# A first windowed attention with its keys ahead of its values, two of eight products on GpSimd at first, and normalisation on ScalarE

## The chip, the core and the metric

The kernel runs on one core of a Trainium2 chip. The metric is the device time of one launch in microseconds (us). Engines are named as in the profile: PE is TensorE (PEld its weight loads), DVE VectorE, ACT ScalarE, POOL GpSimd, SP SyncE, which here only issues transfers. Each engine works through its own list of instructions in order; semaphores tie the lists together.

## The reference, cut to what matters

Four blocks follow each other: a windowed cross attention, a small mixture of adapters, a latent attention and a routed mixture of experts. The change lies in the first block alone:

```python
def _L0_xattn_ref(x, cond, Wq, bq, Wk, bk, Wv, bv, Wo, bo):   # x, cond: (32, 64, 512) = (B, C, T)
    q = _pointwise(Wq, bq, x); k = _pointwise(Wk, bk, cond); v = _pointwise(Wv, bv, cond)
    k = jnp.pad(k, ((0, 0), (0, 0), (8, 7))); v = jnp.pad(v, ((0, 0), (0, 0), (8, 7)))
    idx = jnp.arange(T)[:, None] + jnp.arange(16)[None, :]
    k_win = k[:, :, idx].reshape(B, H, hd, T, W); v_win = v[:, :, idx].reshape(B, H, hd, T, W)
    dots = jnp.einsum('bhdt,bhdtw->bhtw', qh, k_win) * scale      # H = 8, hd = 8, W = 16
    attn = jax.nn.softmax(dots, axis=-1)
    out = jnp.einsum('bhtw,bhdtw->bhdt', attn, v_win)
    return _pointwise(Wo, bo, out.reshape(B, C, T))
x = x + jnp.tanh(g_xattn[0]) * _L0_xattn_ref(_layernorm(x), ctx_4096, ...)
```

## The kernel before, in words

`window_attention` holds x as 16 tiles of 128 rows (two batches of 64 channels) by 512 positions. Group 0 is tiles 0 to 7, group 1 tiles 8 to 15. A unit is one group at a quarter of the positions (T4 = 128), so there are 8 units, 0 to 7; four use group 0. Per unit:

- PE makes the queries (`queries`, L367, 4 matmuls) in PSUM: one half of a bank for the even tiles, one for the odd. ACT adds the bias, the even half in place in PSUM (L284), the odd half into the SBUF tile `q_p` (L287).
- DVE multiplies queries with shifted keys for the 4 even pairs of shifts (L523, `made`), reading PSUM and SBUF; POOL does the 4 others (L230, `pool_made`), reading only SBUF. They fill the 8 slots of `prod[:, m]`, for the quads m = 0 to 3.
- PE sums over the head's channels (`reduce_dots`, L388, even then odd half); ACT copies the result into `attn` (`take_dots`, L299); DVE takes the running maximum (`peak_of`, L539) and subtracts it (`shift`, L545 and L546, all operands in SBUF); ACT takes the exponential (L304); POOL sums over the window (L236 to L241), DVE inverts (L553), POOL multiplies (L246, `normalise_attn`).
- PE spreads the weights over the head's channels (`spread_attn`, L400, couples (m, k)); DVE multiplies them with shifted values (`weighted`, L533) into `prod[:, m]`; PE multiplies with the output weights (`project(u, m, w, n)`, L367 out_ps, n slices from w); DVE adds into x (`add_out`, L562).

The software pipeline is written out by hand. In round v the engines make the dots of unit v and spread, weigh and project unit u = v - 1, with the last of unit v - 2 in front. The query, dot and spread results share three PSUM banks (`ring_ps`); the list `uses` hands them out, and `take` waits until the one before has been read. Keys and values (`keys_values`, `keep`, L278) are made for group 0 at the start, key and value in turn, and for group 1 inside round 3 (`KV_AFTER`), where DVE also normalises tiles 8 to 15 (`normal`, L104). The context tiles pass through four buffers `cond`, filled by SP (L213) and at first by ACT (L268). PE begins when five small loads (`w_in`) are in: weights, `sel`, `ident`, biases and gates. Statistics of x (L495 to L508) and all 8 normalised tiles of group 0 come before the first queries.

## Time and profile before

| | us |
|---|---|
| median of 3 runs | 1569.11 (1568.35 to 1573.99) |
| the profiled execution's own time | 1558.55 |
| its span | 1556.8 |
| PE, DVE, ACT, POOL busy in the span | 1320.9, 811.0, 420.0, 320.4 |
| first attention, start to last product on PE | 0 to 421.5 |

The busy times are sums over all four blocks, and say little of the first one; the windows below cut it at the moments when the queries of a unit are ready. What an engine waits for, and for how long, stands in brackets at the end of a timeline row. The trace counts each matmul of this kernel twice (an x8 in a row is 4 matmuls of the program).

### The profile page before, as it was taken

The numbers are of one execution on the slowest core, as the hardware profiler recorded it, in microseconds if no ns is written. First come the engines' busy times: TensorE is split into PE (matmuls) and PEld (weight loads), VectorE is DVE, ScalarE is ACT, GpSimd is POOL, SyncE is SP. The second block draws the span as 40 slices with busy tenths as digits, with TensorE's granted clock in tenths as the row PEclk, the third lists the DMA queues.
The fourth block names the chain that finished last, engine by engine and source line by source line (L and its number), as shares of the span: only waits on it lengthen the run. The fifth ranks groups of instructions, "written<-read, shape, count | busy, mean of one in ns | idle before, by whom it ended". The sixth has DMA issues, their size and how long they took to land. (4 is left out here: it accounts for less than half of the span.)

```text
span 1556.8 us, 18857 instructions
## 1 busy us (share of the span) xinstructions
PE 1320.9 (85%) x5849; PEld 655.8 (42%) x5850; DVE 811.0 (52%) x1774; ACT 420.0 (27%) x1161; POOL 320.4 (21%) x194
## 2 busy tenths in 40 slices
PE   4477888888788999899998999899996999899950
PEld 1022222222264555455553555455553333477730
DVE  4577868888674156703573156703575451122224
ACT  4201122111033243223342243223343100144420
POOL 3726536656000000000000000000000025232236
PEclk9679999999989999999999999999998998699985
DMA  5000000000060010001000010000004800355647
GB/s 202 0 1 1 1 28 1 1 1 1 1 244 1 1 28 1 2 0 27 0 0 1 0 27 0 1 0 0 0 0 159 324 0 11 124 164 170 166 149 242
DMA packets 44928, 81.02 MB, mean 52 GB/s; under 512 B 21441, under 2 KB 22177, under 8 KB 44338
## 3 DMA queue, kind: packets, MB, share of 16 engines
q1 hardware_dynamic: 34450, 45.50, 8.6%
q0 software_dynamic: 7424, 21.00, 5.1%
q10 hardware_dynamic: 2976, 13.64, 2.2%
q8 instruction: 30, 0.49, 0.1%
q14 instruction: 48, 0.39, 0.1%
HBM read 59.10 MB, written 21.01 MB: 51 GB/s over the span
## 5 line engine op out<-in xcount | busy, mean ns | idle before, releaser
L1151 POOL DMA_INDIRECT table<-ids,slot_of x32 | 30.9, 965 | 897.4 <-DVE slot_of L1362 887.9
L926 PE MATMUL big_ps<-wo_sb,ot 128*128 128x512 f32 x384 | 176.2, 594 | 7.6 <-DVE ot L1040 7.6
L533 DVE TENSOR_TENSOR prod<-ring_ps,v_c 128x1024 f32<-128x1024 f32 x128 | 151.7, 1215 | 43.1 <-PE ring_ps L400 42.8
L917 PE MATMUL big_ps<-ht,wq_sb 128*128 128x512 f32 x384 | 171.4, 592 | 0.0
L883 ACT ACTIVATE probs<-s_ps,npeak 128x128 f32<-128x128 f32 x256 | 91.6, 362 | 270.1 <-PE p_ps L973 233.3
L230 POOL TENSOR_TENSOR prod<-q_p,k_c 128x2048 f32<-128x2048 f32 x32 | 133.4, 4202 | 82.4 <-ACT q_p L287 82.4
L400 PE MATMUL ring_ps<-attn,sel 32*128 32x512 f32 x512 | 100.4, 675 | 47.2 <-DVE prod L533 31.1
L367 PE MATMUL out_ps<-prod,w 64*64 64x512 f32 x1024 | 130.5, 629 | 0.0
L388 PE MATMUL ring_ps<-prod,sel 128*32 128x512 f32 x512 | 72.7, 668 | 34.3 <-POOL prod L230 17.2
L917 PEld LDWEIGHTS big_ps<-ht,wq_sb 128*128 128x128 f32 x384 | 70.1, 190 | 73.9 <-issue 72.8
L926 PEld LDWEIGHTS big_ps<-wo_sb,ot 128*128 128x128 f32 x384 | 68.0, 190 | 72.9 <-issue 65.2
L996 DVE COPY v<-big_ps 128x384 f32<-128x384 f32 x32 | 17.8, 557 | 152.0 <-PE big_ps L909 152.0
L1497 PE MATMUL u_ps<-wr,xgt 128*128 x384 | 92.7, 385 | 0.0
L1038 DVE COPY ot<-o_ps 96x192 f32<-96x192 f32 x128 | 44.5, 348 | 89.9 <-PE o_ps L980 89.6
L1040 DVE COPY ot<-o_ps 32x64 f32<-32x64 f32 x384 | 84.6, 220 | 5.1
L909 PE MATMUL big_ps<-wv_sb,ht 128*128 128x384 f32 x256 | 85.9, 486 | 0.0
L961 PEld LDWEIGHTS s_ps<-kt,qt 96*128 96x128 f32 x512 | 76.8, 191 | 20.1 <-ACT qt L863 8.4
L944 PE MATMUL big_ps<-ht,wk_sb 128*128 128x512 f32 x192 | 85.1, 603 | 0.0
L980 PE MATMUL o_ps<-probs_t,v 128*96 128x256 f32 x256 | 78.5, 388 | 5.2 <-ACT probs_t L891 2.3
L961 PE MATMUL s_ps<-kt,qt 96*128 96x128 f32 x512 | 78.4, 275 | 5.1 <-ACT qt L863 5.1
L523 DVE TENSOR_TENSOR prod<-ring_ps,k_c 128x2048 f32<-128x2048 f32 x32 | 72.4, 2288 | 19.3 <-ACT ring_ps L284 14.8
L1017 DVE TENSOR_REDUCE npeak<-s_ps 128x2 f32<-128x256 f32 x128 | 54.2, 423 | 50.8 <-PE s_ps L961 47.0
(193 smaller groups left out, 1811.8 us busy)
## 6 DMA issues: line engine op xcount, KB each, us to landing
wr<-in_w_routed ACTq DMA_DIRECT2D x4, 3072.0 KB, 21.4
y_rows<-y_sb SPq DMA_DIRECT2D x48, 256.0 KB, 2.0
X<-in_x SPq DMA_DIRECT2D x4, 1024.0 KB, 7.3
ht<-in_ctx_t SPq DMA_DIRECT2D x16, 256.0 KB, 4.9
out<-X SPq DMA_DIRECT2D x16, 256.0 KB, 2.8
cond<-in_ctx SPq DMA_DIRECT2D x12, 256.0 KB, 2.9
wq_sb<-in_wq SPq DMA_DIRECT2D x1, 3072.0 KB, 14.7
wo_sb<-in_wo SPq DMA_DIRECT2D x1, 3072.0 KB, 21.7
```

Source lines behind the costliest of these rows:

```text
L230: nc.gpsimd.tensor_tensor(prod[:, m, 4:8], over_shifts(q_p[:], 4), shifts(k_c, 1, 4, v % 4, m), ALU.mult).then_inc(pool_made, 1)
L367: last = nc.tensor.matmul(out[rows[1 - b if crossed else b], :], w_sb[rows[b], w, rows[b]], rhs[rows[b]], start=start, stop=stop)
L400: last = nc.tensor.matmul(bank("b", u, m, k)[:, j, :], spread[strip, k // 2, :], attn[strip, u % 2, 4 * m:4 * m + 4, :], start=True, stop= ...
L533: V.tensor_tensor(prod[:, m, 2 * k:2 * k + 2], bank("b", u, m, k)[:, :, :].rearrange("p j (w t) -> p j w t", w=4), shifts(v_c[:, u // 4], ...
L883: nc.scalar.activation(probs[:, u % 3, g2, :], s_ps[u % 2][:, g2 * P:(g2 + 1) * P], ACT.Exp, bias=npeak[:, u % 3, g2:g2 + 1], accum_out=to ...
L909: last = nc.tensor.matmul(ps[:, 0:KV * HD1], ht[:, c, b], wv_sb[:, c, :], start=(c == 0), stop=(c == CH - 1))
L917: last = nc.tensor.matmul(ps[:, :], wq_sb[:, c, (a * HC + k) * P:(a * HC + k + 1) * P], ht[:, c, :, 1, :], start=(c == 0), stop=(c == CH - 1))
L926: last = nc.tensor.matmul(ps[:, :], ot[:, a % 2, c, k * P:(k + 1) * P], wo_sb[:, a * HC + c, :], start=(c == 0), stop=(c == HC - 1))
L944: last = nc.tensor.matmul(ps[:, :], wk_sb[:, c, k // 2 * P:(k // 2 + 1) * P], ht[:, c, k % 2 * 4:k % 2 * 4 + 4], start=(c == 0), stop=(c = ...
L961: last = nc.tensor.matmul(s_ps[u % 2][:, g2 * P:(g2 + 1) * P], qt[:, a % 2, b, 2 * g2:2 * g2 + 2], kt[:, a, b], start=True, stop=True)
L1040: last = nc.vector.tensor_copy(ot[HD1:P, a % 2, c, t], heads[c * PIECE:(c + 1) * PIECE, HC])
L1497: last = nc.tensor.matmul(u_ps[m % 2][:, 0:2 * INTER], xgt[:, m % 2, c, :], wr[:, bass.ds(e, 1), c * 2 * INTER:(c + 1) * 2 * INTER], start ...
```

## The change

1. **Start.** SP issues weights, x tiles 0 to 7, and then the whole context of group 0 in four transfers into `first_cond`, which is `prod[:, 3]` under another name; then `sel`, `ident`, four tiles of group 1's context, x tiles 8 to 15. ACT issues only biases and gates. PE waits for the weights alone. It makes four key products, the queries of unit 0, and then the four values; a new wait keeps DVE and POOL off `prod[:, 3]` until the values are made (`kv_done` 8).
2. **Normalisation.** DVE normalises only the first 128 columns of tiles 0 to 7 (xn_ready); ACT does the other 384 with scale and a new `minus_mean` after the values are kept, and all of tiles 8 to 15 between the `take_dots` of unit 3.
3. **Units 0 and 1.** POOL takes 2 of the 8 pairs (128x1024), DVE the other 6: a 128x2048 product and an extra 128x1024 product from PSUM (`made_extra`). ACT biases the odd half in two pieces.
4. **Round 1.** `invert(0)` and `sum_up(0)` change places with a product, and the `shift` of unit 1 comes before the weighted products of unit 0.
5. **Every round from 1.** Slices of `project` move: two slices of m = 1 each time where one stood, then one slice of m = 2, the last spread, the next queries, and only then the second slice of m = 2.

```diff
-            for n in range(4, TILES):
-                if n == PAIRS: ...
-                sp.wait_ge(kv_done, n // 2 * 2 - 2)
-                sp.dma_start(cond[:, n % 4, :], ctx[n]).then_inc(cond_in[n % 4], 16)
+            for i in range(4):
+                sp.dma_start(first_cond[:, 2 * i:2 * i + 2, :],
+                             ctx[2 * i:2 * i + 2].rearrange("t p d -> p t d")).then_inc(first_in[i], 16)
...
@@ gpsimd
-                nc.gpsimd.tensor_tensor(prod[:, m, 4:8], over_shifts(q_p[:], 4), shifts(k_c, 1, 4, v % 4, m),
-                                        ALU.mult).then_inc(pool_made, 1)
+                if v == 0 and m == QUADS - 1:
+                    pool.wait_ge(kv_done, 8)
+                n = 2 if v < 2 else 4
+                nc.gpsimd.tensor_tensor(prod[:, m, 8 - n:8], over_shifts(q_p[:, 4 - n:4], n),
+                                        shifts(k_c, 9 - 2 * n, n, v % 4, m), ALU.mult).then_inc(pool_made, 1)
...
@@ scalar
+            def normal(t, first):
+                nc.scalar.activation(xn[:, t % PAIRS, first:], X[:, t, first:], ACT.Identity, bias=minus_mean[:, t:t + 1],
+                                     scale=rstd[:, t:t + 1]).then_inc(rest_ready, 1)
             root(0)
             for i in range(4):
                 keep("k", 0, i)
+            queries(0)
+            for i in range(4):
                 keep("v", 0, i)
-            queries(0)
+            for t in range(PAIRS):
+                normal(t, T4)
...
@@ tensor
             for i in range(4):
                 keys_values("k", 0, i)
+            queries(0)
+            for i in range(4):
                 keys_values("v", 0, i)
-            queries(0)
...
                 other_keys_values(2, 1)
-                project(u, 1, 0, 1)
+                project(u, 1, 0, 2)
                 spread_attn(u, (2, 3), (3, 0))
                 other_keys_values(2, 3)
-                project(u, 1, 1, 1)
+                project(u, 1, 2, 2)
                 spread_attn(u, (3, 1), (3, 2))
                 other_keys_values(3, 1)
-                project(u, 1, 2, 2)
                 project(u, 2, 0, 1)
                 spread_attn(u, (3, 3))
                 if v + 1 < UNITS:
                     queries(v + 1)
+                project(u, 2, 1, 1)
...
@@ vector
+                if v < 2:
+                    dve.wait_ge(q_ready, 2 * v + 2)
+                    extra = bank("q", v)[:, 1, 0:2 * T4].rearrange("p (j t) -> p j t", j=2)
+                    V.tensor_tensor(prod[:, m, 4:6], over_shifts(extra, 2), shifts(k_c, 1, 2, v % 4, m), ALU.mult)\
+                     .then_inc(made_extra, 1)
...
-                    for m in range(1, QUADS):
-                        dot_products(v, m)
+                    dot_products(v, 1)
+                    dot_products(v, 2)
                     invert(0)
+                    dot_products(v, 3)
                     for m in range(1, QUADS):
                         peak_of(v, m)
+                    shift(v)
+                    dve.wait_ge(kv_ready, 8)
                     weighted(u, 0, 0, 1, 2, 3)
-                    shift(v)
...
-                    if v == 3:
-                        if m == 1:
-                            dve.wait_ge(q_done, 4)
-                        for t in ((8, 9, 10), (11, 12, 13), (14, 15))[m - 1]:
-                            normal(t)
```

At the start of PE's list the group's context was multiplied in one run (cond, 8 products of 4 matmuls), before:

```order
L367 MATMUL ring_ps<-cond,w 64x512 x32
L367 MATMUL ring_ps<-xn,w 64x512 x4
L388 MATMUL ring_ps<-prod,sel 32x512 x24
L367 MATMUL ring_ps<-xn,w 64x512 x4
L388 MATMUL ring_ps<-prod,sel 32x512 x40
```

Now (the prod read by L399 is `first_cond`):

```order
L399 MATMUL ring_ps<-prod,w 64x512 x16
L399 MATMUL ring_ps<-xn,w 64x512 x4
L399 MATMUL ring_ps<-prod,w 64x512 x16
L428 MATMUL ring_ps<-prod,sel 32x512 x24
L399 MATMUL ring_ps<-xn,w 64x512 x4
L428 MATMUL ring_ps<-prod,sel 32x512 x40
```

The queries of unit 0 stand after 16 matmuls in place of 32. On DVE, the dots of units 0 and 1 stood so before:

```order
L523 TENSOR_TENSOR prod<-ring_ps,k_c 128x2048
L539 TENSOR_TENSOR peak<-ring_ps,peak 128x512
L545 TENSOR_TENSOR peak<-peak 128x256
L545 TENSOR_TENSOR peak<-peak 128x128
L546 TENSOR_TENSOR attn<-attn,peak 128x2048
L523 TENSOR_TENSOR prod<-ring_ps,k_c 128x2048 x3
L553 RECIPROCAL inverse<-total 128x128
L539 TENSOR_TENSOR peak<-ring_ps,attn 128x512
L539 TENSOR_TENSOR peak<-ring_ps,peak 128x512 x2
L533 TENSOR_TENSOR prod<-ring_ps,v_c 128x1024 x4
```

Now, from the last product of unit 1's first quad (L564 and L568 are its two pieces) to the shift of unit 1:

```order
L568 TENSOR_TENSOR prod<-ring_ps,k_c 128x1024
L585 TENSOR_TENSOR peak<-ring_ps,peak 128x512
L591 TENSOR_TENSOR peak<-peak 128x256
L591 TENSOR_TENSOR peak<-peak 128x128
L592 TENSOR_TENSOR attn<-attn,peak 128x2048
L564 TENSOR_TENSOR prod<-ring_ps,k_c 128x2048
L568 TENSOR_TENSOR prod<-ring_ps,k_c 128x1024
L564 TENSOR_TENSOR prod<-ring_ps,k_c 128x2048
L568 TENSOR_TENSOR prod<-ring_ps,k_c 128x1024
L599 RECIPROCAL inverse<-total 128x128
L564 TENSOR_TENSOR prod<-ring_ps,k_c 128x2048
L568 TENSOR_TENSOR prod<-ring_ps,k_c 128x1024
```

Each quad costs DVE a second instruction, and the reciprocal stands one quad earlier. On PE, the last part of round 2 (spreads of unit 1, its projections, the queries of unit 3) stood so before:

```order
L367 MATMUL out_ps<-prod,w 64x512 x16
L400 MATMUL ring_ps<-attn,sel 128x512 x8
L367 MATMUL out_ps<-prod,w 64x512 x4
L400 MATMUL ring_ps<-attn,sel 128x512 x4
L367 MATMUL out_ps<-prod,w 64x512 x4
L400 MATMUL ring_ps<-attn,sel 128x512 x4
L367 MATMUL out_ps<-prod,w 64x512 x12
L400 MATMUL ring_ps<-attn,sel 128x512 x2
L367 MATMUL ring_ps<-xn,w 64x512 x4
L400 MATMUL ring_ps<-attn,sel 128x512 x2
L367 MATMUL out_ps<-prod,w 64x512 x8
```

Now:

```order
L399 MATMUL out_ps<-prod,w 64x512 x16
L440 MATMUL ring_ps<-attn,sel 128x512 x8
L399 MATMUL out_ps<-prod,w 64x512 x8
L440 MATMUL ring_ps<-attn,sel 128x512 x4
L399 MATMUL out_ps<-prod,w 64x512 x8
L440 MATMUL ring_ps<-attn,sel 128x512 x4
L399 MATMUL out_ps<-prod,w 64x512 x4
L440 MATMUL ring_ps<-attn,sel 128x512 x2
L399 MATMUL ring_ps<-xn,w 64x512 x4
L399 MATMUL out_ps<-prod,w 64x512 x4
L440 MATMUL ring_ps<-attn,sel 128x512 x2
L399 MATMUL out_ps<-prod,w 64x512 x8
```

The 12 matmuls of projection that stood right ahead of the last spread and the queries are 4 now; 4 each have moved behind the two spreads before, and 4 behind the queries.

## Rows read from the trace of the kernel before

**Rows 1.** Windows by unit: PE, PEld, DVE, ACT, POOL busy (instructions), PE clock, DMA
```profile
47.86:115.24 67.38, 41.58 (x212) 9.86 (x212) 48.60 (x48) 8.71 (x10) 35.38 (x14) 0.71 0.00 1
162.60:222.02 59.42, 46.18 (x330) 12.84 (x328) 46.03 (x37) 14.43 (x17) 26.32 (x9) 0.94 0.05 18
222.02:262.77 40.75, 35.64 (x266) 9.53 (x264) 34.83 (x29) 5.52 (x9) 26.01 (x9) 1.00 0.01 2
...
348.37:421.50 73.13, 65.73 (x502) 18.42 (x500) 55.09 (x50) 4.86 (x7) 26.01 (x9) 1.00 0.00 1
```
**Rows 2.** Windows of 2 us at the start, same columns, last GB/s
```profile
10.00:12.00 2.00, 0.00 (x0) 0.00 (x0) 0.38 (x4) 0.00 (x0) 0.00 (x0) 1.00 1.04 392
...
24.00:26.00 2.00, 1.93 (x20) 0.55 (x12) 0.00 (x0) 1.73 (x2) 0.00 (x0) 1.00 1.04 395
```
**Rows 3.** Timeline: start us, us, engine, line, operation, count, [idle before <-releaser]
```profile
12.59 2.47 DVE L495 BATCH_NORM_STATS2 bn<-X 128x6 f32<-128x512 f32 x4 [2.18 <-DMA X<-in_x]
...
13.18 6.65 PE L367 MATMUL ring_ps<-cond,w 64*64 64x512 f32 x32 [13.18 <-DMA ident<-in_ident_in]
...
16.20 3.74 DVE L104 TENSOR_SCALAR xn<-X,mv,rstd 128x512 f32<-128x512 f32 x8
...
26.28 0.66 ACT L284 ACTIVATE ring_ps<-ring_ps,b 128x512 f32<-128x512 f32 x1
...
27.03 6.69 DVE L523 TENSOR_TENSOR prod<-ring_ps,k_c 128x2048 f32<-128x2048 f32 x3 [6.97 <-ACT ring_ps L284]
...
47.95 2.29 DVE L523 TENSOR_TENSOR prod<-ring_ps,k_c 128x2048 f32<-128x2048 f32 x1 [5.29 <-ACT ring_ps L284]
```
**Rows 4.** Timeline of DVE in unit 1
```profile
50.87 2.13 DVE L545 TENSOR_TENSOR peak<-peak 128x256 f32<-128x256 f32 x1
...
53.04 4.15 DVE L545 TENSOR_TENSOR peak<-peak 128x128 f32<-128x128 f32 x1
...
82.06 0.69 DVE L539 TENSOR_TENSOR peak<-ring_ps,peak 128x512 f32<-128x512 f32 x1 [7.91 <-ACT attn L299]
...
115.28 6.88 DVE L523 TENSOR_TENSOR prod<-ring_ps,k_c 128x2048 f32<-128x2048 f32 x3 [0.51 <-ACT ring_ps L284]
```
**Rows 5.** Timeline: DVE's normalisation in unit 3
```profile
188.16 4.75 DVE L104 TENSOR_SCALAR xn<-X,mv,rstd 128x512 f32<-128x512 f32 x3
...
200.98 5.55 DVE L104 TENSOR_SCALAR xn<-X,mv,rstd 128x512 f32<-128x512 f32 x3
...
216.80 0.99 DVE L104 TENSOR_SCALAR xn<-X,mv,rstd 128x512 f32<-128x512 f32 x2
```
**Rows 6.** Timeline: the last part of unit 4, the first of unit 5
```profile
253.03 1.14 PE L400 MATMUL ring_ps<-attn,sel 32*128 32x512 f32 x8 [0.38 <-DVE prod L533]
...
256.09 1.14 PE L400 MATMUL ring_ps<-attn,sel 32*128 32x512 f32 x8 [0.91 <-DVE prod L533]
257.16 2.81 PE L367 MATMUL out_ps<-prod,w 64*64 64x512 f32 x24
...
260.95 1.09 PE L367 MATMUL ring_ps<-xn,w 64*64 64x512 f32 x8
...
262.81 6.88 DVE L523 TENSOR_TENSOR prod<-ring_ps,k_c 128x2048 f32<-128x2048 f32 x3 [0.51 <-ACT ring_ps L284]
...
282.37 0.68 DVE L539 TENSOR_TENSOR peak<-ring_ps,peak 128x512 f32<-128x512 f32 x1
```
**Rows 7.** Groups by shape, first 430 us: busy, mean ns, idle before
```profile
L533 DVE TENSOR_TENSOR prod<-ring_ps,v_c 128x1024 f32<-128x1024 f32 x128 | 151.7, 1215 | 43.1 <-PE ring_ps L400 42.8
L230 POOL TENSOR_TENSOR prod<-q_p,k_c 128x2048 f32<-128x2048 f32 x32 | 133.4, 4202 | 82.4 <-ACT q_p L287 82.4
...
L546 DVE TENSOR_TENSOR attn<-attn,peak 128x2048 f32<-128x2048 f32 x8 | 18.3, 2292 | 0.3
...
L307 ACT ACTIVATE X<-X,gated_bias 128x512 f32<-128x512 f32 x16 | 10.3, 716 | 0.0
...
L278 ACT ACTIVATE k_c<-ring_ps,b 128x1024 f32<-128x1024 f32 x8 | 8.9, 1111 | 3.2 <-PE ring_ps L367 3.1
```

More of the change, by code:

```diff
@@ L133, in window_attention @@
         peak = sb("peak", [P, WINDOW // 4, T4])
+        minus_mean = sb("minus_mean", [P, TILES])
         total, inverse = sb("total", [P, T4]), sb("inverse", [P, T4])
@@ L141, in window_attention @@
                     (2, 3): (("v", 2), ("k", 3)), (3, 1): (("v", 3),)}
-        uses = [((k, 0, i), 0) for i in range(4) for k in "kv"]
-        uses += [(("q", 0), 0), (("d", 0, 0), 0), (("d", 0, 1), 0), (("q", 1), 1)]
+        uses = [(("k", 0, i), 0) for i in range(4)] + [(("q", 0), 0)]
+        uses += [(("v", 0, 0), 0), (("v", 0, 1), 0), (("v", 0, 2), 1), (("v", 0, 3), 1)]
+        uses += [(("d", 0, 0), 1), (("d", 0, 1), 1), (("q", 1), 1)]
         for v in range(1, UNITS + 1):
@@ L171, in bank @@
             return ring_ps[bank_of[use]]
-        kv_at = {key: n for n, key in enumerate([(k, g, i) for g in range(2) for i in range(4) for k in "kv"])}
-        w_in, x_in, cond_in = sem("w_in"), [sem(f"x_in{k}") for k in range(4)], [sem(f"cond_in{k}") for k in range(4)]
+        kv_order = [(k, 0, i) for k in "kv" for i in range(4)] + [(k, 1, i) for i in range(4) for k in "kv"]
+        kv_at = {key: n for n, key in enumerate(kv_order)}
+        w_in, bias_in, sel_here = sem("w_in"), sem("bias_in"), sem("sel_here")
+        x_in, first_in, cond_in = ([sem(f"{n}{k}") for k in range(4)] for n in ("x_in", "first_in", "cond_in"))
         pads, tanh_done, bias_ready, x_biased = sem("pads"), sem("tanh_done"), sem("bias_ready"), sem("x_biased")
@@ L371, in keys_values @@
             def keys_values(k, g, i):
-                n = g * PAIRS + 2 * i
-                for j in range(2):
-                    pe.wait_ge(cond_in[(n + j) % 4], 16 * ((n + j) // 4 + 1))
+                if g == 0:
+                    pe.wait_ge(first_in[i], 16)
+                    even, odd = first_cond[:, 2 * i, :], first_cond[:, 2 * i + 1, :]
+                else:
+                    for j in range(2):
+                        pe.wait_ge(cond_in[2 * (i % 2) + j], 16 * (i // 2 + 1))
+                    even, odd = cond[:, 2 * (i % 2), :], cond[:, 2 * (i % 2) + 1, :]
                 ps = take(k, g, i)
-                both(ps[:, 0, :], ps[:, 1, :], 1 + (k == "v"), cond[:, n % 4, :], cond[:, (n + 1) % 4, :]).then_inc(kv_done, 1)
+                both(ps[:, 0, :], ps[:, 1, :], 1 + (k == "v"), even, odd).then_inc(kv_done, 1)
             def queries(v):
-                if v % 4 == 0:
-                    pe.wait_ge(xn_ready, PAIRS * (v // 4 + 1))
+                if v == 0:
+                    pe.wait_ge(xn_ready, PAIRS)
+                else:
+                    pe.wait_ge(rest_ready, PAIRS * (v // 4 + 1))
                 ps = take("q", v)
@@ L386, in reduce_dots @@
                 pe.wait_ge(pool_made if odd else made, 4 * v + m + 1)
+                if odd and v < 2:
+                    pe.wait_ge(made_extra, 4 * v + m + 1)
                 for j in range(4):
```

75 lines of the change are left out of this document (48 added, 27 removed).

## The prediction, written before the changed kernel ran

> **What bounds the kernel now.** I read first the windows by unit [rows 1]. The first attention takes 421.5 us of the 1556.8 us span and nothing behind it is edited, so the sum is made in it. Three kinds of stretch stand there. Units 4 and 5 take 40.75 us each; PE is busy for 35.64 and DVE for 34.83 of it, so neither is full: they hand work to and fro. Unit 3 takes 59.4 us and unit 1 67.4 us, with PE busy for 46.2 and 41.6 and a mean granted clock of 0.94 and 0.71 (1.2 GHz is 0.5, 2.4 GHz is 1). These have most idle time.
>
> Then the timeline at the start [rows 3]. The queries of unit 0 stand behind eight key and value products, and those behind a DMA wait that ends at 13.18 with `ident`. DVE waits 6.97 us for ACT and begins its products at 27.03. In unit 1 [rows 4] the shift of unit 0 is held up: two small operations take 2.13 and 4.15 us, and DVE's last maximum waits 7.91 us for ACT, PE and POOL behind it. In unit 3 [rows 5] DVE normalises eight tiles in 11.3 us; the last two take 0.99 us, so six of the eight were slowed from about 0.5 to 1.6 us or more while POOL worked. In unit 4 [rows 6] PE waits 0.38 and 0.91 us for DVE's weighted products, and then does 2.81 us of projection ahead of the last spread and the queries for which DVE waits next.
>
> **The change part by part.**
>
> *Start.* Two queues together moved 392 GB/s and one alone 395 [rows 2], so one queue for all costs no rate, and what counts is the order of bytes. Before, 3.6 MB were in at 12.6. Now x tiles 0 to 7 and the weights are the first 2.4 MB. By the rate they are in at about 9.4, not 12.59, and the four context parts of 0.52 MB (1.35 us each) at 10.7, 12.1, 13.4, 14.7. PE's first 32 passes took 6.65 us, so a key product takes 1.66 us at the clock of the start: 10.8 to 17.4 for four, and the queries are ready on PE at 18.6. Normalisation keeps pace: from the landing to the first tile were 3.6 us [rows 3]; plus 0.2 for `minus_mean` and eight tiles of 128 columns at 0.2, it ends at 14.8. An eighth of the 3.74 us, 0.47, is the upper bound for a tile, and a quarter of it the lower; both end ahead of the queries. ACT keeps the last keys until 18.7 (1.11 us [rows 7]) and has the even queries at 19.5. First product: 27.03 to 19.5, 7.5 us.
>
> From there DVE has per quad one product at 2.23 us (6.69 for three) and one extra of 128x1024. The nearest row for that is the weighted product, also PSUM times SBUF: 1.215, 1.14 when back to back [rows 7]. Its bounds are that and the whole 2.29 of a 128x2048; I take the lower, since shape and operands are the same. So 3.35 per quad. The first scores wait on ACT behind the values (4 x 1.11) and eight normalisations of 384 columns. Three quarters of 0.716 is 0.54 [rows 7], 4.3 us in all; bounds 2.9 and 5.7. They end at about 29, the second scores leave ACT at 31.6, so DVE stands for 2 us ahead of the fourth quad. The fourth product ends at 35.8, unit 0's last scores are out at 37.5, two bias operations later (1.3) ACT biases the queries of unit 1: ready at 39.5. Its product starts at 39.6 and not at 47.95: **8.4 us** gained.
>
> ScalarE's cost is stated by the Trainium skill (page ScalarE: Activation LUTs, Rules for kernel authors) as about 0.3 us plus 0.83 ns an element. By that an operation of 384 columns takes 0.62 us, eight take 5.0, and this term would be 0.7 us smaller; the row of 716 ns for 512 columns agrees with the rule's 0.72.
>
> *Unit 1.* Before, 47.95 to 82.75, 34.8 us. Now DVE has four quads (13.4), four maxima (0.69 each [rows 4], 2.8), the reciprocal (1.0, an estimate: an eighth of the elements of a 128x1024 product, but a division) and the shift (2.3 [rows 7], with its two small parts 3.0). POOL's instructions are half as long, 2.1 in place of 4.2 (bounds 2.1 and 4.2), and a small part is held until the one running ends, so the two wait 1.0 and 1.9 us. With 1.2 us until the query's second half and the sum of unit 0 are there, and 2.5 us of waiting for the last scores, it ends 25.0 us later, at 64.6: **9.8 us** gained. Should a held operation be passed over by POOL, this falls by 2.
>
> The cause is seen in the rows: operations of 128x256 and 128x128 take 2.13 and 4.15 us beside POOL, products with one operand in PSUM keep 2.23. The Trainium skill (page SBUF - State Buffer, Who interferes with whom) says that a `tensor_tensor` with both inputs in SBUF and GpSimd's reads shut each other out for a whole instruction. By that rule the extra products, which read PSUM, are free of it, as summed; if they too were held, 2.1 us each for eight would take 17 us back, and no row shows that.
>
> *Rest of round 1.* Before, 82.75 to 115.28 (32.5). The new order makes the shift first, so exponential and sum of unit 1 come early, but they were not late; what is late is PE, at the low clock, whose spreads (1,0) to (1,2) now wait for the weighted products of quad 0. I get 34.5: **2.0 lost**. Queries of unit 2: 16.2 us earlier.
>
> *Projections (round 2 on).* In unit 4, replayed with its own durations [rows 6]: 8 more passes (0.86 us) ahead of the spread at 253.03, of whose time 0.38 was waiting: 253.45. 16 passes behind it end at 256.4, where it was 256.09. Then 8 passes in place of 24 ahead of the last spread, and the queries start at 259.45 and not 260.95. DVE must first weigh its last couple, done at 261.1; its product starts at 261.3, not 262.81: 1.5 us. In the next part POOL's four products (16.8) set the end; DVE's last maximum moved from 282.37 by 1.9, as it stood then behind PE and DVE work of its own. So 1.9 us per round: units 4 and 5 give 3.7, round 6 with the head of 7 gives 1.9 (statistics on DVE hide part of it), round 2 gives 2.0. At the end PE is bound (65.7 of 73.1 us [rows 1]); the waits filled there, 1.3 and 0.8, give 2.1. **9.7 us**.
>
> *Unit 3.* With DVE free of 11.3 us [rows 5], PE's 46.2 us bound it. Through the banks in their order: spread (1,3) at 191.7, (2,1) at 195.3, (2,3) at 200.6, (3,1) at 205.9, (3,3) at 208.8, queries ready on PE at 210.8 and on ACT at 211.5, where they were ready at 222.02 [rows 1]: 10.5, and 0.3 from the head of the round. **10.8 us**. On ACT the eight normalisations (0.72 each) stand between scores 4 to 5 us apart and end ahead of the exponential: hidden. If that cover failed, up to 1.4 us. The waits for context tiles 12 to 15 are on the same products as before.
>
> *Sum*: 8.4 + 9.8 - 2.0 + 9.7 + 10.8 = 36.7. From the profiled execution's 1558.55 (span 1556.8) that is 1521.9. The median of plain runs stood 10.6 above it, so the forecast is **1532.5**.
>
> **Rivals.**
> 1. *PE's clock holds in units 1 and 2.* PE waits less, so 41.6 us of work at a mean of 0.71 might run near 1. Then some 8 us more go, as the low clock doubles a pass (0.21 against 0.10 us, by 6.65 for 32 and 1.93 for 20). For: less idle time. Against: DVE still sets the pace there. 45 us gained: 1524.
> 2. *The moved projections give nothing*: spreads are pushed back by them and DVE's weighted products wait as long as was won. For: each moved slice stands in front of a spread that DVE needs. Against: PE waited there already. 27 us: 1542.
> 3. *The dots of units 0 and 1 become DVE's bound*: extra products at their upper bound (1.1 us more each, eight: 9) and scores held on ACT behind normalisation (another 6). 21 us: 1548.
> 4. *Slower.* In units 4 to 7 the slices moved forward leave PE one longer stop behind the queries, and the granted clock drops there to 1.2 GHz. Each us of work at that level costs another us. The 36.7 us are spent when one whole unit's PE work (35.64) has dropped, and with two the kernel takes 1604. For: unit 1's 0.71 and unit 3's 0.94. Against: units 4 and 5 were granted 1.00 with 5 us of idle time each, and the new order has less.
>
> **How the numbers follow.** Forecast (31 to 42 us) 0.58, rival 1 0.16, rival 2 0.12, rival 3 0.10, rival 4 0.04. The range leaves out rival 4 and the far ends of 1 and 3: 1519 to 1550. A measurement of this kernel can tell about 0.5%, 7.8 us, from no change. Rivals 1 to 3 and the forecast are all beyond it; of rival 4 half is slower by more, a quarter within, so faster 0.96, same 0.02, slower 0.02.
>
> **What would show it.** Start: PE's first product at about 10.8, DVE's first product at 19.5. Unit 1: its first product near 39.6, the two small operations of the shift at 1.4 and 2.2 us, last maximum near 64, unit 2's first product near 99. Unit 3: no L104 on DVE, 48.5 us long. Units 4 and 5: 38.9 us and 2 us less PE waiting. The end of the first attention near 385. Later parts: same lengths as before. It would be wrong if products of 128x1024 from PSUM took clearly more than 1.2 us beside POOL, if the context landed after 17, or if units 4 and 5 stayed at 40.7.

## The result, and the profile of the changed kernel

Four runs of the changed kernel gave a median of 1528.43 us (1521.83 to 1535.02), four of the kernel before on the same chip 1568.73: a ratio of 0.9736 (95% interval 0.9685 to 0.9786). The forecast was 1532.5. The profiled execution of the changed kernel is the longest of its four, 1535.02 (span 1533.2), and that of before lies 10 us under its own median. From profile to profile only 23.5 us are gone, from median to median 40.3. The last product of the first attention on PE ends at 383.3 (expected near 385, before 421.4). I therefore read the first attention, where the change lies, apart from what follows.

The windows by unit, with the columns of [rows 1]:

```profile
39.38:96.65 57.27, 39.02 (x216) 9.24 (x216) 50.59 (x52) 8.86 (x11) 27.45 (x14) 0.76 0.00 1
141.84:191.92 50.08, 46.72 (x332) 12.87 (x328) 34.95 (x29) 20.10 (x24) 26.08 (x9) 0.93 0.07 22
191.92:230.88 38.96, 35.70 (x268) 9.46 (x264) 34.66 (x29) 5.53 (x9) 26.07 (x9) 1.00 0.01 2
269.87:311.95 42.08, 37.41 (x268) 9.76 (x264) 38.62 (x37) 5.53 (x9) 26.06 (x9) 0.96 0.00 1
```

Unit 1 (first row) lost 10 us and POOL's part of it went from 35.38 to 27.45. Unit 3 lost 9.3, and PE is busy for 46.72 of its 50.08: it has by far the most work there now. Unit 4 has PE's same 35.7 us of work in 38.96. Unit 6 (last row) is the one with the statistics on DVE, and its clock is 0.96.

The timeline at the start, which answers to [rows 3]:

```profile
10.01 2.44 DVE L536 BATCH_NORM_STATS2 bn<-X 128x6 f32<-128x512 f32 x4
...
11.34 5.59 PE L399 MATMUL ring_ps<-prod,w 64*64 64x512 f32 x32 [11.34 <-DMA prod<-in_ctx]
...
13.68 2.13 DVE L625 TENSOR_SCALAR xn<-X,mv,rstd 128x128 f32<-128x128 f32 x8
...
18.90 2.29 DVE L564 TENSOR_TENSOR prod<-ring_ps,k_c 128x2048 f32<-128x2048 f32 x1 [2.96 <-ACT ring_ps L296]
...
21.11 1.22 DVE L568 TENSOR_TENSOR prod<-ring_ps,k_c 128x1024 f32<-128x1024 f32 x1
...
23.88 4.89 ACT L325 ACTIVATE xn<-X,minus_mean,rstd 128x384 f32<-128x384 f32 x8
...
28.94 0.59 ACT L314 COPY attn<-ring_ps 128x512 f32<-128x512 f32 x1 [0.17 <-ACT xn L325]
...
31.26 0.69 DVE L585 TENSOR_TENSOR peak<-ring_ps,attn 128x512 f32<-128x512 f32 x1 [2.28 <-ACT attn L314]
...
39.46 2.29 DVE L564 TENSOR_TENSOR prod<-ring_ps,k_c 128x2048 f32<-128x2048 f32 x1 [3.46 <-issue]
```

PE starts at 11.34 (expected 10.8) and DVE's products at 18.90 (19.5). An extra product of 128x1024 out of PSUM takes 1.22 us. ACT's eight normalisations take 0.61 us each. The copy of the first scores begins 0.17 us behind them, and DVE stands 2.28 us for it ahead of its first maximum. Unit 1's first product is at 39.46 (39.6).

The timeline of unit 1 and of the rest of round 1, which answers to [rows 4]:

```profile
40.21 6.66 POOL L244 TENSOR_TENSOR prod<-q_p,k_c 128x1024 f32<-128x1024 f32 x3 [11.81 <-ACT q_p L302]
...
43.52 3.50 DVE L591 TENSOR_TENSOR peak<-peak 128x256 f32<-128x256 f32 x2
47.05 2.29 DVE L592 TENSOR_TENSOR attn<-attn,peak 128x2048 f32<-128x2048 f32 x1
...
63.98 0.69 DVE L585 TENSOR_TENSOR peak<-ring_ps,peak 128x512 f32<-128x512 f32 x1 [1.98 <-ACT attn L314]
...
74.48 4.74 PE L399 MATMUL out_ps<-prod,w 64*64 64x512 f32 x32
...
96.69 2.29 DVE L564 TENSOR_TENSOR prod<-ring_ps,k_c 128x2048 f32<-128x2048 f32 x1 [0.51 <-ACT ring_ps L296]
```

The two small operations of the shift take 3.50 us together (expected 1.4 and 2.2), beside POOL instructions of 2.2. The last maximum ends at 64.67 (64.6), and waits 1.98 us where it waited 7.91. A 32-pass projection takes 4.74 us at a mean granted clock of 0.76, where 3.66 is the time at full clock. Unit 2's first product is at 96.69 (99).

### The profile page after: what moved, and what is told of

It reads as the page before. It is cut to its first block and busy times, and to the rows that moved or that the text cites. A ratio compares the mean times of both kernels' runs of the same rounds, so it can differ in the third digit from the quotient of the medians.

```text
span 1533.2 us, 18890 instructions
## 1 busy us (share of the span) xinstructions
PE 1322.0 (86%) x5849; PEld 656.1 (43%) x5850; DVE 804.3 (52%) x1776; ACT 430.3 (28%) x1179; POOL 302.9 (20%) x194
## 5 line engine op out<-in xcount | busy, mean ns | idle before, releaser
L244 POOL TENSOR_TENSOR prod<-q_p,k_c 128x2048 f32<-128x2048 f32 (+1 forms) x32 | 117.9, 3715 | 66.2 <-ACT q_p L302 66.0
L399 PE MATMUL out_ps<-prod,w 64*64 64x512 f32 x1024 | 130.2, 623 | 0.0
L564 DVE TENSOR_TENSOR prod<-ring_ps,k_c 128x2048 f32<-128x2048 f32 x32 | 72.1, 2284 | 14.1 <-ACT ring_ps L296 6.1
```

Of the source, the lines that this page charges most:

```text
L244: nc.gpsimd.tensor_tensor(prod[:, m, 8 - n:8], over_shifts(q_p[:, 4 - n:4], n), shifts(k_c, 9 - 2 * n, n, v % 4, m), ALU.mult).then_inc(po ...
L399: last = nc.tensor.matmul(out[rows[1 - b if crossed else b], :], w_sb[rows[b], w, rows[b]], rhs[rows[b]], start=start, stop=stop)
```

## The experiments

All are single edits of the changed kernel unless said otherwise. I compare the end of the first attention, which is the issue of the first route load on SyncE's queue: 428.69 before, 390.65 in the changed kernel, 391.92 in a second profile of it. Two profiles of one kernel, of which there are two pairs, agree to 1.3 and 1.7 us there. Differences below 2 us are therefore read from the place of the edit alone, and that has a spread too: in the six profiles whose edit does not touch the start, unit 1's queries are ready between 38.4 and 39.9. The end also holds short drops of the granted clock, of 1.6 or 3.3 us, that come and go: eleven profiles have the new order of projections, and in seven of them one of units 4 and 5 has such a drop (mean granted clock 0.96 or 0.92, 40.6 or 42.3 us in place of 39.0). The first profile of the changed kernel has none there, so where an experiment has one, it is named below. Ratios are to the kernel before, measured on the same chip in the same batch.

**The old order of projections.**

```diff
-                    project(old, 2, 2, 2)
+                    project(old, 2, 1, 2)
-                    project(old, 3, 0, 1)
+                    project(old, 2, 3, 1)
-                    project(old, 3, 1, 1)
+                    project(old, 3, 0, 2)
...
+                    project(old, 2, 1, 1)
...
-                project(u, 1, 0, 2)
+                project(u, 1, 0, 1)
...
-                project(u, 1, 2, 2)
+                project(u, 1, 1, 1)
...
+                project(u, 1, 2, 2)
-                project(u, 2, 1, 1)
-            project(UNITS - 1, 2, 2, 2)
+            project(UNITS - 1, 2, 1, 3)
```

> The changed kernel with PE's order of projections as before (one slice ahead of each spread, three ahead of the last one and the queries); all else as changed. In the changed kernel's trace the first attention ends at 390.65 us (start of the next block's first load). Theory: each round from 2 on loses the 1.5 to 1.9 us that the moved slices gave, units 4 and 5 go back from 38.97 to 40.75 us, the end comes at 400.3 (9.7 later). Rival (the moved slices give nothing, the spreads were only pushed back): 390 to 393.

Measured: end at 404.93, 14.3 us later; ratio 0.9823 (0.9776 to 0.9871). Units 4 and 5 took 42.50 and 42.43, which is longer than in the kernel before. Unit 4 and one projection in it:

```profile
193.06:235.56 42.50, 37.28 (x266) 9.88 (x264) 34.75 (x29) 5.51 (x8) 26.08 (x9) 0.96 0.00 1
215.49:220.80 5.31, 5.31 (x38) 1.53 (x36) 4.45 (x4) 1.91 (x1) 2.24 (x1) 0.68 0.00 0
```

The same projection in the changed kernel:

```profile
213.88:217.54 3.66, 3.66 (x38) 1.19 (x36) 3.66 (x4) 1.91 (x1) 0.58 (x1) 1.00 0.00 0
```

The granted clock was 0.68 in that stretch and not 1.00, and the 1.65 us by which the projection is longer are most of what unit 4 has above its 40.75 of before. I repeated the kernel to see whether this belongs to it.

> The same kernel as the first experiment (projections in the order of before), once more. Its first attention ended at 404.93 us, 14.3 later than the changed kernel's, where 9.7 was expected, and units 4 and 5 took 42.5 us each, with a short drop of PE's clock in every unit, where the kernel before took 40.75 with none. If the drops belong to this order and its timing, they are there again and the end is near 405; if they come and go from run to run, units 4 and 5 take 40.75 and the end is near 400.5.

Measured: end at 406.66, 16.0 later (against the first profile of the changed kernel); ratio 0.9853 (0.9785 to 0.9921). Unit 4 again took 42.51, unit 5 now 40.80, and a drop stood behind unit 6 instead. So the drops come and go between executions, and the old order without one gives the 40.8 of before. Against the lengths of the kernel before, the first profile has drops of 1.75, 1.66 and 1.76 us (in units 4 and 5 and behind unit 6), the second of 1.76 and 3.45 (in unit 4 and behind unit 6), 5.2 us in each. Without them, undoing the order costs 9.1 and 10.8 us.

**The projections alone, in the kernel before** (the edit above the other way round, nothing else).

> The kernel before with only the new order of projections on PE. Theory: units 4 and 5 at 38.9 in place of 40.75, the first attention 9.7 us shorter than 428.69, ending at 419, if PE's clock drops as often. Rival (the new order needs the rest of the change): less than 3 us shorter.

Measured: end at 413.50, 15.2 us earlier than before; ratio 0.9900 (0.9845 to 0.9955).

```profile
157.06:214.51 57.45, 46.83 (x332) 13.01 (x328) 45.96 (x37) 14.44 (x17) 26.31 (x9) 0.94 0.06 19
214.51:253.41 38.90, 35.67 (x268) 9.37 (x264) 34.76 (x29) 5.53 (x9) 26.01 (x9) 1.00 0.00 1
```

Unit 4 (second row) is at 38.90, as summed. The 15.2 fall on round 1 with 1.9, unit 2 with 3.6, unit 3 (first row) with 2.0, units 4 and 5 with 3.7, unit 6 with 2.3 and the rest with 1.7. In this pair of profiles the part is worth 15, not 9.7: it also pays in round 1 and in unit 3, where I had not booked it under this head, and in unit 2 more than I had booked. Undone in the changed kernel it was worth 9.1 and 10.8 without the drops. Its size is open between 9 and 15; that it pays 1.8 to 1.9 us a unit is shown by units 4 and 5 of the undisturbed profiles.

**GpSimd with four of eight pairs again in units 0 and 1.**

```diff
-                n = 2 if v < 2 else 4
+                n = 4
...
-                if v < 2:
-                    nc.scalar.activation(odd[:, 0:2 * T4], odd[:, 0:2 * T4], ACT.Identity, bias=b_sb[:, 0:1])
...
-                    V.tensor_tensor(prod[:, m, 4:6], over_shifts(extra, 2), shifts(k_c, 1, 2, v % 4, m), ALU.mult)\
-                     .then_inc(made_extra, 1)
```

> The changed kernel with POOL doing four of the eight pairs in units 0 and 1 too (no extra products on DVE). Theory, by the hold-up of operations with both operands in SBUF: the two small parts of unit 0's shift wait for POOL operations of 4.2 us (together 6 us, not 3.5), the large part starts 4 to 7 us later than 47.05, unit 1's last maximum ends near 70 (64.67 now) and the first attention near 398. Rival (the gain of unit 1 comes from the order of round 1 alone): under 2 us later than 390.65.

Measured: end at 400.57, 9.9 later; ratio 0.9786 (0.9727 to 0.9846). Unit 1 took 64.95 us and began 1.7 later, so unit 2's queries were ready 9.4 later. Behind that, a drop in unit 4 (40.60 us) added 1.6, and other units gave back 1.1. The shift of unit 0 on DVE:

```profile
44.10 6.33 DVE L580 TENSOR_TENSOR peak<-peak 128x256 f32<-128x256 f32 x2
50.47 6.14 DVE L581 TENSOR_TENSOR attn<-attn,peak 128x2048 f32<-128x2048 f32 x1
```

POOL beside it:

```profile
41.77 12.69 POOL L244 TENSOR_TENSOR prod<-q_p,k_c 128x2048 f32<-128x2048 f32 x3 [4.61 <-ACT q_p L300]
```

POOL's three products run from 41.77 to 54.46, at 4.2 us each. The two small operations take 6.33, and the large subtraction 6.14: it ends at 56.61, which is 2.15 behind the third product, so it was held until that had ended. In the changed kernel POOL's three short products end at 46.87 and the subtraction, from 47.05, takes its bare 2.29. That is 12.5 us in place of 5.8. The Trainium skill (page SBUF — State Buffer, Who interferes with whom) says that operations with both inputs in SBUF and GpSimd's reads shut each other out: these rows agree. By the same rule the changed kernel's extra products, which read PSUM, are free of it. They are: the first of them, at 21.11, took 1.22 us while POOL's products ran from 19.71 to 28.40, as it did anywhere else.

**VectorE normalises in unit 3 again.**

```diff
-                    if v == 3:
-                        if m == 0:
-                            act.wait_ge(shift_ready, 2)
-                            act.wait_ge(q_done, 4)
-                        normal(PAIRS + 2 * m, 0)
-                        normal(PAIRS + 2 * m + 1, 0)
...
+                    if v == 3:
+                        if m == 1:
+                            dve.wait_ge(q_done, 4)
+                        for t in ((8, 9, 10), (11, 12, 13), (14, 15))[m - 1]:
+                            normalise(nc, xn[:, t % PAIRS, :], X, t, mv, rstd).then_inc(rest_ready, 1)
```

> The changed kernel with tiles 8 to 15 normalised on DVE in round 3, as before, and not on ACT. Theory: six of the eight operations are held by POOL again (about 10 us on DVE in place of 4), unit 3 takes 57 to 59 us in place of 50.1, the first attention ends near 399. Rival (unit 3 is bound by PE's key and value products anyway): under 2 us later than 390.65.

Measured: end at 397.69, 7.0 later; unit 3 took 58.48; ratio 0.9826 (0.9775 to 0.9877). The normalisation on DVE:

```profile
165.58 4.76 DVE L104 TENSOR_SCALAR xn<-X,mv,rstd 128x512 f32<-128x512 f32 x3
...
178.41 5.56 DVE L104 TENSOR_SCALAR xn<-X,mv,rstd 128x512 f32<-128x512 f32 x3
...
194.82 0.99 DVE L104 TENSOR_SCALAR xn<-X,mv,rstd 128x512 f32<-128x512 f32 x2
```

These are the rows of before [rows 5] to 0.01 us, and unit 3 is back at nearly its old length. By itself this edit is worth 7.0 to 8.4 us, the second figure by unit 3 alone.

**Values between keys again** (`k` and `v` products by turns, queries of unit 0 last; the loads of the change kept).

```diff
-        uses = [(("k", 0, i), 0) for i in range(4)] + [(("q", 0), 0)]
-        uses += [(("v", 0, 0), 0), (("v", 0, 1), 0), (("v", 0, 2), 1), (("v", 0, 3), 1)]
-        uses += [(("d", 0, 0), 1), (("d", 0, 1), 1), (("q", 1), 1)]
+        uses = [((k, 0, i), 0) for i in range(4) for k in "kv"]
+        uses += [(("q", 0), 0), (("d", 0, 0), 0), (("d", 0, 1), 0), (("q", 1), 1)]
```

> The changed kernel with keys and values of group 0 made in turn and the queries of unit 0 behind all eight, as before; loads, normalisation and everything else as changed. Theory: DVE's first product moves from 18.90 to 24 us (4 more products at 1.66 and less), but the first scores stand behind ACT's normalisation, which ends at nearly the same time, so the first product of unit 1 moves only from 39.46 to 42.2 and the end of the first attention by 2.7, to 393.4. Rival (the queries' lead is worth all of itself): 5 us later, 395.7.

Measured: end at 392.37, 1.7 later; ratio 0.9765 (0.9716 to 0.9814).

```profile
22.12 2.29 DVE L561 TENSOR_TENSOR prod<-ring_ps,k_c 128x2048 f32<-128x2048 f32 x1 [6.63 <-ACT ring_ps L295]
...
39.98 2.29 DVE L561 TENSOR_TENSOR prod<-ring_ps,k_c 128x2048 f32<-128x2048 f32 x1 [3.13 <-issue]
```

The products start 3.2 us later, but unit 1 only 0.5. Keys ahead of values is nearly worthless as it stands: what DVE gains at its first product it gives back ahead of the maximum, behind ACT's normalisation (a wait of 2.28 us in the changed kernel, none here). The 1.7 us of the end are no loss of this order either: unit 2's queries were ready 1.2 us earlier, and unit 5 had a drop (42.33 us, 3.3 more).

**VectorE normalises all of group 0.**

```diff
-            for t in range(PAIRS):
-                normal(t, T4)
...
-                V.tensor_scalar(xn[:, t, 0:T4], X[:, t, 0:T4], mv[:, t, 0:1], rstd[:, t:t + 1], ALU.subtract,
-                                ALU.mult).then_inc(xn_ready, 1)
+                normalise(nc, xn[:, t, :], X, t, mv, rstd).then_inc(xn_ready, 1)
```

> The changed kernel with tiles 0 to 7 normalised whole on DVE before the first queries (3.7 us in place of 2.1), nothing of them on ACT. Theory: the first queries start 0.8 us later, but the first scores no longer stand behind 4.9 us of normalisation on ACT, and DVE's stop of 2.3 us ahead of its first maximum goes, so that unit 1's first product comes 1.5 us earlier than 39.46 and the first attention ends near 389. Rival (ACT's share pays, as it takes 1.6 us off the path to the first queries): 1 us later, 391.7.

Measured: end at 387.05, 3.6 *earlier*; ratio 0.9771 (0.9703 to 0.9839).

```profile
25.25 0.59 ACT L314 COPY attn<-ring_ps 128x512 f32<-128x512 f32 x1 [1.16 <-PE ring_ps L425]
...
36.87 2.29 DVE L561 TENSOR_TENSOR prod<-ring_ps,k_c 128x2048 f32<-128x2048 f32 x1 [3.12 <-issue]
```

The first scores leave ACT at 25.25 and not at 28.94, and unit 1 starts 2.6 us sooner, while DVE's first product moved from 18.90 only to 19.01. So that part of the change costs 2.6 us at unit 1's first product: it took work off DVE at a time when DVE was waiting for PE. How much of it reaches the end is open. At unit 2's queries 1.2 are left; units 2 and 3 were then 2.7 and 1.3 shorter, and a drop in unit 4 took 1.6.

**ACT's normalisation dealt out between the scores, and bias operations moved to unit 1.**

```diff
-            for t in range(PAIRS):
+            for t in range(2):
...
+                    if v == 0 and m == 3:
+                        queries(1)
...
+                    if v == 0 and m < 2:
+                        for t in range(2 + 3 * m, 5 + 3 * m):
+                            normal(t, T4)
```

> A version meant to be faster: the changed kernel with ACT's list of unit 0 in another order. Scores of quads 0 and 1 are taken between the normalisations (2, 3 and 3 tiles), the queries of unit 1 get their bias ahead of the last scores, and the output bias is added in unit 1. Theory: DVE's stop of 2.3 us ahead of its first maximum and the one of 3.5 us ahead of unit 1 go; unit 1's first product at 34 in place of 39.46 and the first attention ends 5 to 6 us earlier, near 385. Rival (PE or POOL takes over in unit 1): under 2 us earlier.

Measured: end at 388.15, 2.5 earlier; median 1524.15, ratio 0.9690 (0.9615 to 0.9765).

```profile
33.63 2.29 DVE L567 TENSOR_TENSOR prod<-ring_ps,k_c 128x2048 f32<-128x2048 f32 x1
...
243.84 3.73 PE L443 MATMUL ring_ps<-attn,sel 32*128 32x512 f32 x12 [1.52 <-DVE peak L588]
...
247.51 5.25 PE L402 MATMUL out_ps<-prod,w 64*64 64x512 f32 x32
```

Unit 1's first product is at 33.63, 5.8 us sooner, and unit 2's queries 7.2 sooner. Then 4.7 are given back, 3.3 in unit 5 and 1.3 in unit 6. Unit 5 took 42.30 and not 38.99. Its twelve-pass spread took 3.73 us and the projection behind it 5.25, where 3.66 is the time at full clock; the granted clock in these 8.9 us was 0.61:

```profile
243.84:252.70 8.86, 8.86 (x46) 3.06 (x46) 6.30 (x6) 1.91 (x1) 3.71 (x3) 0.61 0.01 2
```

**The same, and one more slice of projection behind a spread.**

```diff
-                project(u, 0, 0, 4)
+                project(u, 0, 0, 3)
...
+                project(u, 0, 3, 1)
```

> A version meant to be faster: the kernel with scores taken between normalisations, and in each round the fourth slice of the projection of quad 0 moved behind the spread (1,3), (2,0). Theory: PE's wait of 1.4 us per round is partly filled and DVE's 0.3 us goes, 0.3 us per round and 2 us in all; units 4 and 5 at 38.7 without a drop of PE's clock, unit 2's first product at 89.5, end between 381 and 386, by how often the clock drops. Rival (DVE sets these parts alone): 38.96, end as the version it starts from.

Measured: end at 382.75, the earliest of all; units 4 and 5 took 38.82 and 38.84. The slice is worth 0.14 us a unit (0.3 was expected); the rest is the edit above without its drop in unit 5, though with one of 1.6 behind unit 6. The median of 1518.64 (ratio 0.9708, 0.9660 to 0.9757) is the lowest in its batch, 12 us under the repeat of the changed kernel there. The intervals of the two overlap, so in whole time it is likely faster, not shown to be. In the first attention its gain is 8 to 9 us between single profiles.

**Round 1 in the old order** (three dot products ahead of the reciprocal, weighted products ahead of the shift).

```diff
-                    dot_products(v, 1)
-                    dot_products(v, 2)
+                    for m in range(1, QUADS):
+                        dot_products(v, m)
...
-                    dot_products(v, 3)
...
-                    shift(v)
...
+                    shift(v)
```

> The changed kernel with round 1 in its old order: the reciprocal of unit 0 behind all products of unit 1 on DVE, the sum and the normalisation on POOL one product earlier, and the shift of unit 1 behind the weighted products of quad 0. Theory: normalisation of unit 0 ends later (reciprocal at 60 in place of 56.5) and the first spread with it, end of the first attention 1.5 us later, 392.2. Rival (this order is what gained unit 1): 5 us or more later.

Measured: end at 391.31, 0.7 later, which is within what two profiles differ by; ratio 0.9806 (0.9748 to 0.9864). Unit 2's queries were ready at 100.16 and not at 96.65, which is 3.5 later. Units 2 and 3 were then 2.7 and 1.4 shorter, and a drop in unit 4 (40.58 us) took 1.6. Unit 2's length differs by as much among the other experiments (42.5 to 45.2 us), and unit 3 was short here because it had no drop. So nothing shows that the edit itself gives the 3.5 back, and nothing shows that it keeps it: its worth stays open between 0 and 3.5 us.

**The loads as before** (`sel` and `ident` ahead of the context, and the context on two queues).

```diff
-            for i in range(4):
-                sp.dma_start(first_cond[:, 2 * i:2 * i + 2, :],
-                             ctx[2 * i:2 * i + 2].rearrange("t p d -> p t d")).then_inc(first_in[i], 16)
...
+            for i in range(2):
+                act.dma_start(first_cond[:, 2 * i:2 * i + 2, :],
+                              ctx[2 * i:2 * i + 2].rearrange("t p d -> p t d")).then_inc(first_in[i], 16)
...
+            pe.wait_ge(sel_here, 32)
```

> The changed kernel with its first loads as before: half of the group's context from ACT's queue beside the x tiles on SP's, and PE waiting for sel and ident too. Theory: the first key product starts at 13.2 and not at 11.34, the second half of x lands 2.6 us later and the normalised tiles with it, first product on DVE at 21, unit 1's at 41.5, end of the first attention 2.1 us later, 392.8. Rival (loads are hidden behind ACT's normalisation): under 0.7 us later.

```profile
13.54 5.06 PE L403 MATMUL ring_ps<-prod,w 64*64 64x512 f32 x32 [13.54 <-DMA ident<-in_ident_in]
...
20.95 2.29 DVE L567 TENSOR_TENSOR prod<-ring_ps,k_c 128x2048 f32<-128x2048 f32 x1 [2.04 <-ACT ring_ps L299]
```

PE starts 2.2 us later, DVE 2.05, unit 1 1.7. That is the worth of this edit at the start; at unit 2's queries 0.75 of it is left. The end is at 396.18, 5.5 later, of which 4.6 are drops in units 5 and 6 (42.3 and 43.4 us); ratio 0.9826 (0.9772 to 0.9881).

**The changed kernel again, in five rounds.** The profile behind the first attention had asked for it. Between the load of `xt` and the first rows of the routed block, the changed kernel:

```profile
1281.54:1332.11 50.57, 44.60 (x88) 17.91 (x87) 8.40 (x16) 4.63 (x12) 7.75 (x9) 0.56 0.27 84
```

and the kernel before:

```profile
1320.11:1356.46 36.35, 30.23 (x73) 14.49 (x73) 6.02 (x12) 4.63 (x12) 7.80 (x9) 0.58 0.38 116
```

This piece of unedited code took 14.2 us more, and PE was busy for 14.4 more in it. But it is not the same work: 88 matmul records lie in it and 73 before. The load that marks its start does not wait for all of PE's work ahead of it, and PE was further behind by then. From the first load of the routed block to the first rows, where both profiles have the same 396 matmul records, it is 185.3 us against 171.7, 13.7 more, with PE busy for 153.1 and 148.7. PE had stood still ahead of the load, and its granted clock was 0.50 from then to 1321:

```profile
1279.68 0.57 ACT L1226 COPY gt<-y_ps 17x512 f32<-17x512 f32 x1 [24.36 <-remote]
...
1280.40 2.05 PE L1289 MATMUL y_ps<-w_sb,h_sb 128*128 128x512 f32 x2 [9.54 <-ACT gt L1226]
```

Either the change makes this part longer, or its length changes by chance.

> The changed kernel itself once more, for its first attention against its whole time. Theory: the first attention again ends within 1.5 us of 390.65, the stretch of the routed block's shared part that ran 51 us at PE's low clock in the first profile has another length here, and the plain runs spread over more than 10 us; their median is 36 to 42 us under the kernel before. Rival (the change itself lengthens the late low stretch, by 14 us): it is 51 us again, and the plain runs are never more than 30 us under the kernel before.

Measured: median 1530.7 against 1566.9; ratio 0.9769 (0.9714 to 0.9823). Between the load of `xt` and the first rows this profile had 41.5 us, but only because the load of `xt` came late, 8.5 us behind the load of the table that stands just ahead of it:

```profile
1282.37 0.32 SPq L1185 DMA_DIRECT2D tab_sb<-table  x1
1290.88 0.35 SPq L1187 DMA_DIRECT2D xt<-in_b_routed  x1
```

From the load of the table it is 50.0 us, as in the first profile (50.9), and from the start of the block 185.1 (185.3). So the changed kernel had the long form twice (and in this profile a drop in unit 5, 40.62 us). Measured from the start of the block, the 14 profiles fall into two groups: 168.9 to 172.2 us (the kernel before; the old projections, second time; projections alone; four pairs on POOL; values between keys; the loads as before) and 181.9 to 185.3 (the eight others). The old projections have one of each, 183.1 and 168.9 us from the same kernel. So one kernel can have both lengths. The plain times of the changed kernel fit that: three of the six lie at 1519 to 1525 us and three at 1536 to 1538. That the change makes the long form more frequent is not excluded by the traces, but the medians, 36 and 40 us apart, show no such loss against the 38.0 of the first attention. What starts the long form is open: waits of the kind shown above, with `remote` as the releaser, stand in profiles of both groups.

## Why the prediction was right, step by step

The mechanism held: the gain is in the first attention, 38.0 us against a sum of 36.7, and no part of it turned into a new wait of its size. The forecast time of 1532.5 lies 4.1 us above the median. It took the distance from the profiled execution to the median, 10.6 us, over from the kernel before; in the changed kernel the profile lies 6.6 above its median and not below it. It had the long form of the routed block, and the profile of before the short one. That the whole time came out so near rests in part on luck. In the sum itself the two largest errors, 2.5 us too little for the rest of round 1 and 1.5 too much for unit 3, partly cancel. The terms, as measured between the two profiles:

| term | forecast | profiles | undone or done alone |
|---|---|---|---|
| start to unit 1's first product | 8.4 | 8.5 | loads 1.7, keys first 0.5, ACT normalising −2.6 |
| unit 1 to its last maximum | 9.8 | 9.6 | four pairs on POOL 9.4 (units 0 and 1) |
| rest of round 1 | −2.0 | +0.5 | order of round 1: 0 to 3.5 |
| projections, without unit 3 | 9.7 | 10.1 | 13.2 alone; 9.1 and 10.8 undone without drops, unit 3 within |
| unit 3 | 10.8 | 9.3 | VectorE normalising 7.0 to 8.4 |

*Start.* The total was right by errors that cancel. PE began 0.5 us late, and its first 32 passes took 5.59 us and not 6.65: passes of 0.21 us gave way to passes of 0.12 within them and not behind them. I had called the slow ones the low clock, also in rival 1. That rests on their length alone, as the profile lists a granted clock of 1.00 for this stretch in both kernels; that the lowered clock doubles a pass is shown by the spread of 1.99 and 3.68 us under *Unit 3*. And ACT's eight normalisations took 4.89 and not 4.3: three quarters of the 512-column row is too low, as the cost has a part that doesn't shrink with the columns. The Trainium skill's rule (page ScalarE: Activation LUTs, Rules for kernel authors), 0.3 us plus 0.83 ns an element, gave 0.62 for one; the row has 0.61. The rule was better than my scaling.

*Unit 1.* Extra products took 1.22 (bounds 1.14 to 2.29), the small operations 3.5 together (marks 3.6), and the last maximum ended 0.1 us off its mark. That mark was luck in part: the terms as I listed them add up to 26.8 us and not to the 25.0 that I wrote, and 25.2 was measured, as the waits were shorter (0.46 us in place of 1.2 ahead of the reciprocal, 1.98 in place of 2.5 for the last scores). Rival 3 falls with its larger half: the extra products stayed at the row of same shape and operands. Its smaller half, scores held on ACT behind normalisation, is there in part, with the 2.6 us that VectorE normalising group 0 gives back.

*Rest of round 1.* A mis-sized term. I let PE run at the low clock throughout, but this stretch had a mean granted clock of 0.82 already before (0.84 now), and 32 passes took 4.74 us at 0.76. That the assumed clock made up all of the 2.5 us between −2.0 and +0.5 is argued, not measured. Over unit 1 the clock rose from 0.71 to 0.76: rival 1 came in a small part, and no run puts a price on it.

*Projections.* By the places I had booked, the profiles give 10.1 for 9.7: units 4 and 5 3.6 (3.7), round 2 2.2 (2.0), unit 6 with the end 4.3 (4.0). Alone it gives 13.2 beside the 2.0 in unit 3. Round 1 had no entry in my sum, and unit 2 gains 3.6 there and 2.2 between the two profiles; a replay of one full-clock unit was not enough for the stretches in which the clock changes. Rival 2 is refuted: with the old slices, a unit without a drop is back at 40.80.

*Unit 3.* 9.3 and not 10.8. The timeline has the cause, a twelve-pass spread at a lowered clock; the first row is the same spread one unit earlier:

```profile
116.69 1.99 PE L440 MATMUL ring_ps<-attn,sel 32*128 32x512 f32 x12 [1.52 <-DVE peak L585]
...
148.75 1.52 ACT L325 ACTIVATE xn<-X,minus_mean,rstd 128x512 f32<-128x512 f32 x2
...
161.89 3.68 PE L440 MATMUL ring_ps<-attn,sel 32*128 32x512 f32 x12 [1.52 <-DVE peak L585]
```

After the same wait of 1.52 us the spread took 1.99 us in unit 2 and 3.68 in unit 3, as it took 3.73 in the disturbed unit 5 above. The middle row shows ACT's normalisation at 0.76 us a tile; it stayed hidden, as said. Two experiments that leave unit 3 as it is had no drop in it, and it then took 48.73 and 48.78 us, where 48.5 had been expected. Unit 3 of the run with round 1 in its old order, and the spread in it:

```profile
142.65:191.38 48.73, 43.54 (x332) 12.04 (x328) 34.94 (x30) 20.10 (x24) 26.06 (x9) 1.00 0.06 22
162.67 1.99 PE L440 MATMUL ring_ps<-attn,sel 32*128 32x512 f32 x12 [1.52 <-DVE peak L585]
```

So the term itself was right to about 0.1 us, and 1.35 us were lost in the disturbed unit: PE was busy for 3.2 us more there, and its waits were 1.8 us shorter.

*Units 4 to 7.* The order at the end of unit 4, which answers to [rows 6]:

```profile
220.02 1.14 PE L440 MATMUL ring_ps<-attn,sel 32*128 32x512 f32 x8 [1.41 <-DVE prod L579]
221.09 1.95 PE L399 MATMUL out_ps<-prod,w 64*64 64x512 f32 x16
...
225.92 1.14 PE L440 MATMUL ring_ps<-attn,sel 32*128 32x512 f32 x8
226.99 1.09 PE L399 MATMUL out_ps<-prod,w 64*64 64x512 f32 x8
228.01 1.13 PE L440 MATMUL ring_ps<-attn,sel 32*128 32x512 f32 x4
229.07 1.09 PE L399 MATMUL ring_ps<-xn,w 64*64 64x512 f32 x8
```

Ahead of the last spread stand 8 passes (1.09 us) in place of 24 (2.81), and the waits of 0.38 and 0.91 for DVE are gone from the later spreads. Rival 4 (the clock drops in whole units) didn't come: units 4 and 5 have 1.00. What it was made of exists, though, as single drops that cost 1.6 to 3.4 us, in the old order as in the new; seven of the eleven profiles with the new order have one in unit 4 or 5. Whether the order changes their number is not shown.

*Later parts.* "Same lengths as before" was wrong for the one profile by the 13.7 us above and right for the medians. Up to the routed block the two profiles agree: 756.1 us in both from the end of the first attention to the first load of that block.

## What to carry to other kernels

Before an operation is moved to an emptier engine, ask whether the engine that loses it was waiting at that moment and what is queued behind it on the engine that gets it: here normalising eight tiles on ACT gained 7 us where DVE was behind and cost 2.6 at the next unit's start where DVE was ahead. Work that fills PE should stand behind the operation for which another engine waits, in every round; an edit of a few lines of order gave 10.1 us between the two profiles, as much as each of the larger edits. Count the drops of the clock in a profile before reading a small difference from its end. And where an unedited stretch has its own chance length, compare profiles piece by piece, begin and end each piece where the same instructions lie between, and compare whole times only by medians.

## What the runs showed of the hardware that was not expected

- The granted clock falls for a few microseconds in units that otherwise have 1.00 (0.68 in 5.31 us, 0.61 in 8.86 us). Two of the drops shown begin at a twelve-pass spread behind a wait of 1.52 us for DVE, but the same spread behind the same wait also ran undisturbed (1.99 us). A unit loses 1.3 to 3.4 us by one, and most profiles of the first attention have one or more.
- From the first load of the routed block to its first rows, the same 396 matmul records took 168.9 to 172.2 us in six profiles (mean granted clock 0.85 to 0.89) and 181.9 to 185.3 in eight (0.80 to 0.83), with both lengths (183.1, 168.9) for one kernel: a spread of some 1% of the whole time without any edit.
- Not only small operations of DVE are held by GpSimd: with POOL instructions of 4.2 us, a subtraction of 128x2048 with both inputs in SBUF took 6.14 us, and 2.29 in the kernel with instructions of 2.2. In the latter case GpSimd's products had just ended, 0.18 us ahead of it: shorter instructions on GpSimd saved twice here, in each stall and in the number of operations that met one. The two small operations took 0.75 us together in unit 1, with GpSimd idle.
